# Linear attention: another engine clips the FFN's weights and makes their signs

## The reference, cut to what matters

```
def _quant_weight(w):
    scale = jnp.mean(jnp.abs(w)) + EPS
    wq = jnp.clip(jnp.round(w / scale), -1.0, 1.0)
    return (wq, scale)

# attention of the first layer, 16 heads of 128
q_big = rope(einsum(q_hk, w_kc_q));  kv_r = rope(kv_c)
scores = einsum(q_big @ W_qr, kv_r @ W_kr)
attn = softmax(scores);  ctx_c = attn @ kv_r
return (ctx_c @ w_kc_kv) @ Wo.T
```

## Time and profile before

| | us |
|---|---|
| median of 3 runs | 1941.34 (1939.52 to 1941.47) |
| the profiled execution | 1943.23 |
| its span, first to last instruction | 1941.4 |

### The profile page before, as it was taken

The page is one execution under the profiler, slowest core; times in us unless marked ns, Lnnn a source line. Parts: engine busy times, 40 slices in busy tenths (PEclk is TensorE's granted clock), DMA queues, the critical chain, the costliest instruction groups (busy, mean ns, idle before and its releaser), DMA issues. The chain is left out here.

```text
span 1941.4 us, 30474 instructions
## 1 busy us (share of the span) xinstructions
PE 1772.2 (91%) x10896; PEld 1408.2 (73%) x10910; DVE 1318.7 (68%) x2912; ACT 913.6 (47%) x2005; POOL 599.5 (31%) x582
## 2 busy tenths in 40 slices
PE   5899999999899999999996998799978989999997
PEld 4677887778777887778773544566655878888896
DVE  6677677776687778887777896477666633444564
ACT  3544445433543445434543554555544324555563
POOL 5332222331633122321211131232231454343353
PEclk9899999999999999999998999799989999999999
DMA  5022112210121222222205111000005167787773
GB/s 212 17 89 86 55 48 73 89 60 33 62 83 37 97 77 71 71 97 85 77 17 206 36 40 39 25 1 2 1 14 178 57 191 220 239 279 269 236 238 77
DMA packets 49671, 188.50 MB, mean 97 GB/s; under 512 B 7388, under 2 KB 11612, under 8 KB 38260
## 3 DMA queue, kind: packets, MB, share of 16 engines
q1 hardware_dynamic: 39396, 166.86, 24.0%
q0 software_dynamic: 9840, 19.70, 5.6%
q10 hardware_dynamic: 288, 0.00, 0.0%
HBM read 158.29 MB, written 28.24 MB: 96 GB/s over the span
## 5 line engine op out<-in xcount | busy, mean ns | idle before, releaser
L437 POOL TENSOR_TENSOR la_q_roped<-la_q_roped 128x400 f32<-128x400 f32 x128 | 134.7, 1074 | 655.8 <-DVE la_q_roped L968 655.8
L861 ACT ACTIVATE la_probs<-banks,la_minus_max 100x361 f32<-100x361 f32 x256 | 144.7, 565 | 176.6 <-DVE la_minus_max L1079 176.6
L968 DVE TENSOR_TENSOR la_q_roped<-banks,la_rope_q 128x400 f32<-128x400 f32 x384 | 198.0, 566 | 35.4 <-PE banks L552 26.6
L606 PEld LDWEIGHTS banks<-identity,la_probs 100*121 100x121 f32 x768 | 111.8, 185 | 79.4 <-DVE la_probs L1086 54.0
L1086 DVE TENSOR_SCALAR la_probs<-la_probs,la_rsum 100x361 f32<-100x361 f32 x256 | 153.9, 601 | 9.1
L645 PE MATMUL banks<-la_ctx_parts,la_wout_high 128*128 128x416 f32 (+3 forms) x512 | 157.9, 360 | 2.2 <-DVE residual L1020 1.9
L606 PE MATMUL banks<-identity,la_probs 100*121 100x100 f32 x768 | 128.2, 276 | 31.3 <-DVE la_probs L1086 18.9
L1079 DVE TENSOR_REDUCE la_minus_max<-banks 100x1 f32<-100x361 f32 x256 | 134.8, 526 | 29.9 <-PE banks L597 27.8
L617 PE MATMUL banks<-la_probs_t,la_kv_rows 121*128 121x200 f32 x768 | 152.4, 334 | 0.0
L2370 DVE TENSOR_TENSOR ex_weights_low<-ex_raw_weights,ex_weights_high 128x2048 fp32r<-128x2048 f32 x39 | 89.4, 2292 | 90.1 <-ACT ex_weights_high L2254 90.1
L879 ACT COPY la_probs_t<-banks 121x300 f32<-121x300 f32 x256 | 104.8, 409 | 64.0 <-PE banks L606 63.7
(11 more groups left out here) (378 smaller groups left out, 5017.1 us busy)
## 6 DMA issues: line engine op xcount, KB each, us to landing
ex_raw_weights<-w_exp SPq DMA_DIRECT2D x39, 1024.0 KB
la_weights<-w_pack SPq DMA_DIRECT2D x15, 1856.0 KB, 8.4
residual<-w_exp SPq DMA_DIRECT2D x24, 1024.0 KB
la_kv_turned<-w_ffn SPq DMA_DIRECT2D x30, 384.0 KB
la_rope_k<-w_ffn SPq DMA_DIRECT2D x30, 384.0 KB, 3.4
qf_sign_weights<-ffn_signs SPq DMA_DIRECT2D x3, 2048.0 KB, 8.0
ffn_signs<-la_ffn_signs SPq DMA_DIRECT2D x30, 192.0 KB, 2.1
out<-ex_block_out POOLq DMA_DIRECT2D x13, 256.0 KB
```

Of the source, the lines that this page charges most:

```text
L437: pool.tensor_tensor(roped[:, h, 0, c, :], roped[:, h, 0, c, :], roped[:, h, 1, 1 - c, :], ALU.add).then_inc(b_add, 1)
L606: mm = pe.transpose(ps[0:LC, T_BANK, c * S:(c + 1) * S], prob[:, j % 4, c * LC:(c + 1) * LC], core.ident[0:S, 0:S])
L861: act.activation(prob[:, s % 4, 0:L], ps[0:S, s % 2, 0:L], ACT.Exp, bias=nmax[:, s % 4:s % 4 + 1], accum_out=sums[:, s % 4:s % 4 + 1]).the ...
L968: dve.tensor_tensor(roped[:, h, v, c, :].rearrange("p (b s) -> p b s", b=GB), ps[:, B_BANKS[k % 2], 0:NT].rearrange("p (b s) -> p b s", b=GB),
```

## The change

Pool gets a routine `signs_of(n, k)` with the two instructions of VectorE's `chunk`, which goes. Pool calls it for the five chunks of pair n-1 behind `split(n)` and ahead of the partners of pair n, and for the three chunks of pair 15 at its end. ScalarE scales all five chunks of a pair in slots 5, 6, 10, 12 and 15, none in the front. SP loads the weights of the next pair but one first, and then waits for the signs, chunk by chunk, stores them and loads new chunks.

```
-        SCALE_AT, SIGN_AT = (8, 13), (9, 14)
+        SCALE_AT = (5, 6, 10, 12, 15)
...
-                def refill_signs(n, which):
-                    for c in chunks_of(n, True)[which]:
+                def refill_signs(n):
+                    for c in chunks_of(n, True):
                         m, lo, width = chunks[c]
                         sp.wait_ge(q_done, c + 1)
                         sp.dma_start(w_quant[m, :, lo:lo + width], signs[:, 0:width]).then_inc(q_out, 16)
...
                 for n in range(2, RUNS + 1):
                     refill_sums(n - 1)
-                    refill_signs(n - 2, slice(3, None))
...
-                        refill_signs(n - 1, slice(0, None))
+                        refill_signs(n - 2)
+                        refill_signs(n - 1)
                         continue
...
-                    refill_signs(n - 1, slice(0, 3))
+                    refill_signs(n - 2)
...
             def _(pool):
+                def signs_of(n, k):
+                    if k >= len(chunks_of(n, True)):
+                        return
+                    c = chunks_of(n, True)[k]
+                    width = chunks[c][2]
+                    w = raw_w[c % 2][:, 0:width]
+                    pool.wait_ge(q_up, c + 1)
+                    pool.tensor_scalar(w, w, ROUND - 1.0, ROUND + 1.0, ALU.max, ALU.min).then_inc(q_clip, 1)
+                    pool.wait_ge(q_clip, c + 1)
+                    if c:
+                        pool.wait_ge(q_out, 16 * c)
+                    pool.tensor_scalar(signs[:, 0:width], w, ROUND, None, ALU.subtract).then_inc(q_done, 1)
...
                 for n in range(1, RUNS):
                     split(n)
+                    for k in range(EACH_SIGN):
+                        signs_of(n - 1, k)
...
                     for u in range(UNITS):
                         partners(n, u)
+                    if n + 1 == RUNS:
+                        for k in range(EACH_SIGN):
+                            signs_of(n, k)
...
             def _(act):
                 def pair(n):
                     summing = len(chunks_of(n, False)) > 0
-                    chunk(n, 0)
                     if summing:
+                        chunk(n, 0)
                         chunk(n, 1)
                     high(n, 2)
-                    chunk(n, 2 if summing else 1)
+                    if summing:
+                        chunk(n, 2)
                     high(n, 3)
...
-                            chunk(n, 3 + SCALE_AT.index(s))
+                            chunk(n, SCALE_AT.index(s))
...
             def _(dve):
-                def chunk(n, k):
-                    ...
-                    dve.tensor_scalar(w, w, ROUND - 1.0, ROUND + 1.0, ALU.max, ALU.min).then_inc(q_clip, 1)
-                    ...
-                    dve.tensor_scalar(signs[:, 0:width], w, ROUND, None, ALU.subtract).then_inc(q_done, 1)
...
                     rope(n, 0, 2)
-                    chunk(n, 0)
                     low(n, 2)
                     rope(n, 1, 0)
                     rope(n, 1, 1)
                     rope(n, 1, 2)
-                    chunk(n, 1)
                     low(n, 3)
...
-                    chunk(n, 2)
...
-                        if s in SIGN_AT:
-                            chunk(n, 3 + SIGN_AT.index(s))
```

More of the change, by code:

```diff
@@ L839, in pair @@
                         chunk(n, 5)
-                    else:
-                        chunk(n, 2)
                     if starts_half(n):
@@ L988, in wout_low @@
                                              op0=ALU.mult, op1=ALU.subtract).then_inc(m_low, 1)
-                def chunk(n, k):
-                    if k >= len(chunks_of(n, True)):
-                        return
-                    c = chunks_of(n, True)[k]
-                    width = chunks[c][2]
-                    w = raw_w[c % 2][:, 0:width]
-                    dve.wait_ge(q_up, c + 1)
-                    dve.tensor_scalar(w, w, ROUND - 1.0, ROUND + 1.0, ALU.max, ALU.min).then_inc(q_clip, 1)
-                    dve.wait_ge(q_clip, c + 1)
-                    if c:
-                        dve.wait_ge(q_out, 16 * c)
-                    dve.tensor_scalar(signs[:, 0:width], w, ROUND, None, ALU.subtract).then_inc(q_done, 1)
                 def total():
```

## The result

| | before | after |
|---|---|---|
| median | 1939.52 us (7 runs) | 1946.48 us (7 runs) |
| ratio, 95% interval | | 1.0038 (1.0028 to 1.0048) |
| the profiled execution | 1943.23 us | 1943.78 us |
| its span | 1941.4 us | 1942.0 us |

What follows compares the result with a forecast made beforehand. TensorE was taken to bound the sign pairs, with some 4 us of gaps. Pairs 9 to 14 add 1.2 us and pair 15 adds 1.2 us: +2.4 us on the median 1941.3 gives 1943.7 us, range 1936 to 1951.

Steps and rivals of the forecast that it cites:

- The likeliest case: Whole kernel: time stays within 0.2%, 3.9 us, of before; chance 0.41.
- the slower side: Whole kernel: slower than even, mostly by Pool holding VectorE's norms; chance 0.35.
- the lock: Slots 5 to 12: Pool's work holds VectorE's norms through the shared port; 0.1 to 0.2 us counted as reaching TensorE.
- Pool's chunk: Pool's clip and sign of one 768-column chunk: 2.1 to 2.2 us, by width from its scalings on 512 columns.
- The gain: Removing VectorE's chunks: 0.75 us in seven fronts and 0.44 us in six slots, at most 7.9 us back.
- ScalarE's order: Scalings in slots 5, 6, 10, 12, 15: about 0.95 us over before in each of pairs 9 to 14.
- Slot 10: nothing: ScalarE's scaling in slot 10: hidden by 1.08 us of idle time ahead of the exponential, so no cost.
- its rival: Four chunks each hold a norm, TensorE loses 0.4 us for each: +8.7 us more, 1952.4 us; chance 0.32.
- the step's reason: Slots: TensorE needs a norm only a slot later, so only 0.1 to 0.2 us was counted.
- my sign for the lock: Profile after: TensorE's gaps at the turnings would be released by the norm's line, L1086.
- that rival's condition: It decides when TensorE loses over 0.1 us a chunk more than counted; 6 x 4 x 0.07 = 1.6 us.
- Pool too late: Pair's end: the fifth chunk runs into the next pair's partners, needing 9 us delay; 1950 us or more, chance 0.03.

Runs made afterwards that it cites:

- Pool works 3.0 us a chunk: Kernel after, with Pool's clip replaced by multiply and add, its sign by a multiplication, so no signs are made; 1942.59 us, 1.0017 of before.
- the one-column run: Kernel before, with VectorE's clip and sign working on one column each, all places as before; 1933.27 us, 0.9963 of before.
- Pool on one column: Kernel after, with Pool's clip and sign working on one column each, ScalarE, SP and waits unchanged; 1940.82 us, 1.0006 of before.
- with 5.2 us: Kernel after, with the constants of Pool's clip and sign taken from one-column SBUF tiles instead of the instruction; 1952.5 us, 1.0063 of before.

## Why the prediction was right, and where it was not

The range of 1936 to 1951 held the result. The likeliest case, even within 0.2%, did not come. It went to the slower side, which had a chance of 0.35, but only in part by the mechanism that carried most of this chance, the lock. Two terms came out too small, Pool's chunk and the lock; that the time stayed in the range is owed to its upper end, which had been set for a far larger lock. The runs give the sum its terms one by one, each run going one step further (ratios times 1939.5 us; each difference uncertain by some 3 us):

| step | from the ratios | from S | forecast |
|---|---|---|---|
| VectorE's work gone | 0.9963: -7.2 us | 388.10: -6.9 us, and 0.8 ahead of S | -7.9 us |
| ScalarE's and SP's new order | to 1.0006: +8.3 us | to 397.70: +9.6 us | +10.3 us, with the next row |
| Pool works 3.0 us a chunk | to 1.0017: +2.1 us | to 398.43: +0.7 us | in the row above |
| Pool works 4.9 us a chunk (late loads and more held norms) | to 1.0038: +4.1 us | to 402.21: +3.8 us | 0 |
| sum | +7.4 us | +6.4 us | +2.4 us |

The traces behind the column of S all have a clock of 1.00 in these pairs.

*The gain was right.* 0.75 us a front and 0.44 us a slot stood for at most 7.9 us; the one-column run gave 7.2. Its pairs 9 to 13 last 60.66 to 60.69 us, in place of 61.61 to 61.89.

*ScalarE's order was right.* Over what could be won, the prediction charged each of pairs 9 to 14 with 0.95 + 0.44 = 1.39 us. With Pool on one column pairs 9 to 13 last 61.89 to 62.09 us, that is 1.2 to 1.4 us over the 60.67, and pair 14 lasts 60.88 us, 1.25 over its 59.63. For pair 15 it charged 2.0 us of cost (1.2 net of the front); the slots of pair 15, first to last maximum, take 26.81 us there and 25.11 with VectorE on one column, 1.7 us more. The two gaps were at the turnings and of the sizes named, and were released by the copy.

*Pool's chunk was mis-sized*, and this is the step that failed: "I take 2.1 to 2.2 us". It is 4.9 us. The earlier trace rows show a product and sum and a product, and I scaled them by width to a maximum and minimum. A product and sum would have been even cheaper than my figure, 0.83 us for 768 columns (the rows have 0.77 for 512, with its factors from a tile); the maximum and minimum cost over three times that. The sentence on the Trainium skill ("GPSIMD Engine Reference", section "Engine selection", roughly line-rate for one-input work, by which I estimated 1.3 us a chunk) lay further off still: no row here is near it but the product and sum.

*"Slot 10: nothing"* fell with it. I costed the scaling there by ScalarE's idle time of 1.08 us, and "the store lands near 701" only for Pool's next sign. I did not follow the chain to its end: sign, store, load, then a scaling of the same tile two chunks on. With 2.2 us a chunk it would have held: at 3.0 us it did. At 4.9 us the load for slot 10 is late where it also lands slowly, by 1.33 us in pair 10; with 5.2 us it is that for slot 12, and its gap brings the clock down.

*The lock* was real, small against its rival, and still larger than I had it. I had counted 0.1 to 0.2 us for it in a pair, and 0.4 us a chunk as the rival. The runs leave 0.7 to 2.1 us over all seven pairs at 3.0 us a chunk, and at 4.9 us at least 1.4 us in all (0.4 us in pair 11 and 0.5 us in pair 12, without a late load). The norms themselves lost 12.3 us more than before (31.5 - 19.2), so most of it stayed hidden: a norm is needed only a slot later, which was the step's reason. What gets through goes by the next maximum, so my sign for the lock, gaps released by the norm, could not show it. (In that rival's condition 6 x 4 x 0.07 is 1.7 us, not 1.6, which changes nothing.)

*Pool too late* did not come. Of the 9 us reserve that the prediction named, 5.8 were left.

## What to carry to other kernels

Before work goes to an engine, find a row with the same operation on it, not only the same size: the price here differed by more than three times between two operations of one form. Follow a moved step through the whole ring of its buffer (compute, store, reload, next user), since a step with ample time on its own engine can still be late for the one that reuses the tile. Look at the granted clock where a time grows by more than its gaps: in four runs here a fall behind gaps of 1.0 to 2.4 us added 1.6 us to a pair. And when an instruction is in the way, try its place before its engine: here moving it on the same engine gave all that removing it could.

## What the runs showed of the hardware that I had not expected

Pool's price goes by the operation and its form. On 128 x 768 elements the maximum with minimum took 2.78 us, a single product or subtraction with a constant 2.13 us, a product with a sum 0.83 us. Constants from a tile added 0.1 to 0.15 us to the clip and the sign, and the output's type nothing (the subtraction took 2.14 us into bf16 and 2.13 into f32). Why a single product with a constant costs more than a product with a sum stays open.

Pool does not hold up VectorE for the whole of such an instruction. Norms that began 0.66, 0.76 and 1.47 us into a clip took their usual 0.41 us; one that began 1.98 us into it waited to its end. With the sign it goes like this (timeline of both engines after, pair 10, each sign of Pool and the norm that began in it):

```profile
699.26 2.14 POOL L488 TENSOR_SCALAR la_ffn_signs<-la_kv_turned 128x768 bf16<-128x768 f32 x1
...
699.49 0.80 DVE L1087 TENSOR_SCALAR la_probs<-la_probs,la_rsum 100x361 f32<-100x361 f32 x1
...
705.67 2.14 POOL L488 TENSOR_SCALAR la_ffn_signs<-la_rope_k 128x768 bf16<-128x768 f32 x1
...
706.33 0.41 DVE L1087 TENSOR_SCALAR la_probs<-la_probs,la_rsum 100x361 f32<-100x361 f32 x1
...
710.75 2.14 POOL L488 TENSOR_SCALAR la_ffn_signs<-la_kv_turned 128x768 bf16<-128x768 f32 x1
...
711.24 0.54 DVE L1087 TENSOR_SCALAR la_probs<-la_probs,la_rsum 100x361 f32<-100x361 f32 x1
```

The norm that began 0.23 us into a sign lost 0.39 us, the one at 0.49 us lost 0.13 us, and the one at 0.66 us nothing: the first two went on 0.62 us into Pool's instruction. The one at 1.31 us (695.49, above) waited to the end. All 26 norms of pairs 9 to 15 that began in a sign fit: the eight within its first 0.49 us went on about 0.62 us into it, the ten at 0.66 to 1.27 us lost nothing, the eight from 1.31 us on waited to the end. So VectorE's norm is shut out at the beginning and at the end of Pool's sign and let in between. Pool's split is different: a norm that began 0.65 us into it waited to its end, 1.2 us later. The Trainium skill ("SBUF — State Buffer", section "SBUF: two separate sides") has the port pair that both share held for the whole instruction; the split agrees with that, but the rows of the clip and the sign do not. It is one reason why Pool's 24 us more in a pair did so little. The durations are the profiler's, and Pool's its least certain ones.
